# Packed tables of tiles and two register sets in the expert loops of a two-layer language-model tower

## The reference

```python
logits = xf @ Wr + br
probs = jax.nn.softmax(logits, axis=-1)
vals, idx = jax.lax.top_k(probs, K)
cw = (jax.nn.one_hot(idx, E, dtype=x.dtype) * vals[..., None]).sum(axis=1)
...
h = jax.nn.relu(xf @ W1e + b1e)
y = h @ W2e + b2e
acc + cwe[:, None] * y
```

## Time and profile before

| | us |
|---|---|
| median of 3 timed runs | 1137.43 |
| their range | 1136.9 to 1138.49 |
| span of the profiled execution | 1221.9 |
| first loop (L638 from 257.7 us on) | about 134 |
| second loop (793 to 1141.6 us) | 348.6 |

### The profile page before, as it was taken

One profiled execution on the slowest core, in us unless ns is written; L12 is line 12 of the kernel. 1 busy time (PEld: TensorE's weight loads), 2 busy tenths in 40 slices (PEclk: granted clock), 3 DMA queues, 4 the chain that ended last, 5 costly groups with the idle time before them and its releaser, 6 DMA issues.

```text
span 1221.9 us, 18019 instructions
## 1 busy us (share of the span) xinstructions
PE 802.4 (66%) x5133; PEld 637.8 (52%) x5133; DVE 778.2 (64%) x2305; ACT 437.9 (36%) x1233; POOL 510.6 (42%) x528
## 2 busy tenths in 40 slices
PE   0218963879998248778587511287887897888343
PEld 0105552679998124434255401177776787777332
DVE  7885467656665248888766699855555555666642
ACT  2543241524444134443103304533343444444200
POOL 7841001255540634662101002466664435555574
PEclk9759965579999556666665555599999998999755
DMA  2290089012221287566400404133332223333222
GB/s 69 76 403 37 1 249 309 1 50 70 71 66 38 60 143 140 118 143 131 77 1 1 132 0 127 33 85 85 89 83 81 83 77 87 88 96 94 59 72 75
DMA packets 116599, 112.95 MB, mean 92 GB/s; under 512 B 16403, under 2 KB 102994, under 8 KB 116258
## 3 DMA queue, kind: packets, MB, share of 16 engines
q1 hardware_dynamic: 103228, 84.68, 25.3%
q0 software_dynamic: 13280, 27.13, 8.2%
HBM read 76.15 MB, written 35.57 MB: 91 GB/s over the span
## 4 chain that ended last, share of the span: by engine, by line
PE 55%; DVE 22%; issue 9%; POOL 5%; ACT 4%; DMA 3%; another core or an unknown queue 1%; SPq 0%; DVEq 0%; POOLq 0%; ACTq 0%
PE ps L638 18%; PE ps L645 15%; DVE wide L1348 6%; PE ps L1969 4%; POOL wide L810 3%; PE ps L633 3%; DVE wide L1229 3%; PE ps L2231 3%; PE ps L2139 2%; PE ps L2180 2%; ACT wide L1757 2%; DVE bnst L955 2%; POOL wide L874 1%; PE ps L2076 1%; PE ps L2224 1%
## 5 line engine op out<-in xcount | busy, mean ns | idle before, releaser
L645 PE MATMUL ps<-big,wide 128*128 x1568 | 238.1, 282 | 33.9 <-ACT wide L605 20.6
L638 PE MATMUL ps<-wide 128*128 (+1 forms) x1580 | 247.1, 287 | 18.9 <-DVE wide L554 12.2
L867 POOL DMA_INDIRECT wide<-xrows,holder x189 | 182.8, 967 | 158.1 <-PE ps L633 116.1
L559 DVE TENSOR_SCALAR wide<-ps,wide 128x128 f32<-128x128 f32 x395 | 131.7, 348 | 156.9 <-PE ps L638 138.4
L638 PEld LDWEIGHTS ps<-wide 128*128 128x128 f32 x1580 | 206.2, 195 | 40.8 <-issue 32.9
L645 PEld LDWEIGHTS ps<-big,wide 128*128 128x128 f32 x1568 | 203.7, 194 | 44.5 <-issue 43.9
L605 ACT ACTIVATE wide<-ps,wide 128x128 f32<-128x128 f32 x395 | 137.8, 367 | 202.4 <-PE ps L638 184.9
L1348 DVE TENSOR_REDUCE wide<-ps 125x3 f32<-125x1500 f32 (+1 forms) x96 | 143.7, 1540 | 46.7 <-PE ps L1969 45.3
L874 POOL DMA_INDIRECT wide<-results,place x128 | 127.6, 997 | 100.1 <-DVE h L1328 44.0
L1969 PE MATMUL ps<-big 97*125 97x500 bf16 x256 | 104.8, 545 | 40.3 <-DVE wide L1348 32.5
L623 ACT COPY wide<-ps 128x128 f32<-128x128 f32 x322 | 85.2, 264 | 92.1 <-PE ps L645 78.1
(11 more groups left out here) (388 smaller groups left out, 1102.7 us busy)
## 6 DMA issues: line engine op xcount, KB each, us to landing
results<-wide SPq DMA_DIRECT2D x161, 128.0 KB, 1.8
big<-kappa SPq DMA_DIRECT2D x8, 1750.0 KB, 21.0
big<-parts SPq DMA_DIRECT2D x96, 125.0 KB
big<-in_L_ffn_W_dram SPq DMA_DIRECT2D x10, 1024.0 KB, 9.4
big<-in_L_ffn_W_dram SPq DMA_DIRECT2D x64, 128.0 KB, 2.6
parts<-wide SPq DMA_DIRECT2D x24, 250.0 KB
xrows<-wide SPq DMA_DIRECT2D x2, 1792.0 KB
wide<-results,place POOLq DMA_INDIRECT x192
```

The lines of the kernel that those rows point to most:

```text
L559: last = v.tensor_scalar(ring.hid[u % 2][:, 128 * k:128 * k + 128], ps[:, 4 + u % 2, 128 * k:128 * k + 128], w[:, hid + k:hid + k + 1], 0. ...
L638: last = t.matmul(ps[:, (2 if k < c.HC // 2 else 4) + u % 2, 128 * k:128 * k + 128], ring.w1[u % U][:, 128 * k:128 * k + 128], turned, sta ...
L645: last = t.matmul(ps[:, 6 + u % 2, 0:D], ring.hid[u % 2][:, 128 * k:128 * k + 128], w[:, D * k:D * k + D], start=k == 0, stop=k == c.HC - 1)
L867: gp.indirect_dma_start(ring.rows[j % RING], None, xrows[:, :], bass.IndirectOffsetOnAxis(ap=holder[:, j:j + 1], axis=0)).then_inc(S(f"row ...
```

## The change

The tables become bytes. PE's has two bytes per tile, the expert's number and the place of the block in the ring, unscaled; VectorE's has one byte per tile, the expert's number alone. Both are written by copies that convert to bytes; the separate scaling and the second column of VectorE's table are gone. The four tables now have places of their own in one tensor.

The loops read the bytes as 32-bit words: four words hold a round of eight tiles for PE, two for VectorE. There are two register sets; in the middle of each round (after the fourth tile on PE, in the third on VectorE) one load brings the next round's words into the set that is not in use. `value` cuts a byte out of its word, by a shift and an AND, and multiplies it by the scale.

```diff
-        table = sb("table", [1, 2 * TAB], I32)
+        table = sb("table", [1, 4 * TAB], U8)
...
         class Words:
...
+            def __init__(self, engine, p, table, tiles):
+                self.engine, self.table, self.tiles = engine, table.bitcast(I32), tiles
+                self.count = table.shape[-1] * RING // (4 * tiles)
+                self.sets = [[engine.alloc_register(f"{p}word{k}_{n}") for n in range(self.count)] for k in range(2)]
+
+            def load(self, turn):
+                at_ = turn * self.count
+                self.engine.reg_load(self.sets[turn % 2], self.table[0:1, at_:at_ + self.count])
+
+            def value(self, tile, byte, scale, top):
+                per = 4 * self.count // RING
+                word, bit = divmod(8 * (tile % RING * per + byte), 32)
+                reg = self.engine.snap(self.sets[tile // RING % 2][word])
+                field = (reg >> bit if bit else reg) & 255
+                return nc.s_assert_within(field * scale, 0, top * scale, skip_runtime_bounds_check_because="the tables hold clipped numbers")
...
-                    stage(words.value(u, 0), u + 3)
-                    if u % 2 and first_tile + u + RING < c.tiles:
-                        words.load(first_tile + RING, u - 1)
+                    if u == DVE_WORDS_AT and first_tile + RING < c.tiles:
+                        words.load(first_tile // RING + 1)
+                    if first_tile + u + 3 < c.tiles:
+                        stage(words.value(first_tile + u + 3, 0, c.wcols, c.E - 1), u + 3)
+                    else:
+                        stage(0, u + 3)
...
-                    first(u + 1, words.value(u, 1))
+                    first(u + 1, words.value(first_tile + u + 1, 1, 128, KEEP[c.n] - 1))
...
-                    second(words.value(u, 0), u)
-                    if u % 2 and first_tile + u + RING < c.tiles:
-                        words.load(first_tile + RING, u - 1)
+                    second(words.value(first_tile + u, 0, c.HC * D, c.E - 1), u)
+                    if u == PE_WORDS_AT and first_tile + RING < c.tiles:
+                        words.load(first_tile // RING + 1)
...
-                me.did(TS(tiles_[:, :, 0], one, float(c.HC * D), None, ALU.mult))
-                me.did(TS(stages_[:, 0:tab - 1, 0], one[:, 1:tab], float(c.wcols), None, ALU.mult))
-                me.then(TS(wrap, numbers, float(keep), -128.0 * keep, ALU.is_ge, ALU.mult))
-                me.did(v.scalar_tensor_tensor(stages_[:, :, 1], numbers, 128.0, wrap, ALU.mult, ALU.add))
+                me.did(v.tensor_copy(tiles_[:, :, 0], one))
+                me.did(v.tensor_copy(stage_tables[f], one))
                 me.settle()
-                me.then(TS(wrap, block, float(keep), -128.0 * keep, ALU.is_ge, ALU.mult))
-                me.then(v.scalar_tensor_tensor(tiles_[:, 0:tab - 1, 1], block[:, 1:tab], 128.0, wrap[:, 1:tab], ALU.mult, ALU.add))
+                me.then(TS(wrap, block, keep, -keep, ALU.is_ge, ALU.mult))
+                me.then(TT(out=tiles_[:, :, 1], in0=block, in1=wrap, op=ALU.add))
```

More of the change, by code:

```diff
@@ L21 @@
 U32 = mybir.dt.uint32
+U8 = mybir.dt.uint8
 ALU = mybir.AluOpType
@@ L94 @@
 KEEP = {0: 32, 1: 67}
+PE_WORDS_AT = 3
+DVE_WORDS_AT = 2
 def ap(t, offset, dims):
@@ L261, in tower_kernel @@
         b1r = sb("b1r", [128, 2, 128])
-        table = sb("table", [1, 2 * TAB], I32)
+        table = sb("table", [1, 4 * TAB], U8)
         w0 = 2 * FFN[0].tab
-        assert 2 * w0 <= 2 * TAB <= 512
-        tile_tables = [table[0:1, 0:w0], cst[0:1, 128:128 + 2 * TAB].bitcast(I32)]
-        stage_tables = [table[0:1, w0:2 * w0], table[0:1, 0:2 * TAB]]
+        assert w0 % 16 == 0 and w0 + FFN[0].tab <= TAB
+        tile_tables = [table[0:1, 0:w0], table[0:1, TAB:3 * TAB]]
+        stage_tables = [table[0:1, w0:w0 + FFN[0].tab], table[0:1, 3 * TAB:4 * TAB]]
         place = [sb("place", [128, 4, NT], I32)] * 2
@@ L457, in weight_loads @@
             return c.E // (8 if c.n else 4) + (W2_EARLY if c.n else 8)
[L459 to L467, removed]
@@ L469, in tower_kernel @@
-        class Words:
[L471 to L482, removed]
+        class Words:
+            def __init__(self, engine, p, table, tiles):
[11 more added lines that the diff above has]
+                return nc.s_assert_within(field * scale, 0, top * scale, skip_runtime_bounds_check_because="the tables hold clipped numbers")
@@ L484, in free @@
             def free(self):
-                for r in self.regs:
+                for r in self.sets[0] + self.sets[1]:
                     self.engine.free_register(r)
@@ L565, in expert_vector @@
             dve.wait_ge(S(f"w{c.n}_ld"), 16 * weight_loads(c))
-            w1, _ = pairs_of(mybir.EngineType.DVE, stage_tables[c.n], 0, 2, (c.E - 1) * c.wcols, (KEEP[c.n] - 1) * 128)
-            words = Words(dve, p, stage_tables[c.n], 2, (c.E - 1) * c.wcols, (KEEP[c.n] - 1) * 128)
+            words = Words(dve, p, stage_tables[c.n], c.tab)
+            words.load(0)
             dve.wait_ge(S("bank_filled"), nfill[at[f"holder{c.n}", len(c.parts) - 1]])
@@ L571, in expert_vector @@
             v.tensor_copy(ring.blocks[:, 0:128], ps[:, 0, 0:128]).then_inc(S(p + "blocks_in"), 1)
-            stage(w1[0], 1)
+            stage(words.value(1, 0, c.wcols, c.E - 1), 1)
             dve.wait_ge(S(p + "turned"), 2)
             v.tensor_copy(ring.blocks[:, 128:256], ps[:, 1, 0:128]).then_inc(S(p + "blocks_in"), 1)
-            stage(w1[1], 2)
+            stage(words.value(2, 0, c.wcols, c.E - 1), 2)
             dve.wait_ge(S(p + "hid_filled"), 3)
@@ L647, in second @@
                 last.then_inc(S(p + "res_filled"), 1)
-            words = Words(pe, p, tile_tables[c.n], 0, (c.E - 1) * c.HC * D, (KEEP[c.n] - 1) * 128)
+            words = Words(pe, p, tile_tables[c.n], c.tab)
+            words.load(0)
             pe.sem_inc(S(p + "hid_filled"), 2)
@@ L1152, in route @@
                 dve.wait_ge(S("emptied_dve"), nth[at[f"expert{f}", 0]])
-                keep = KEEP[f]
+                keep = float(KEEP[f])
                 numbers = tileno[0:1, 0:tab]
-                tiles_, stages_ = (t_.rearrange("o (t w) -> o t w", w=2) for t_ in (tile_tables[f], stage_tables[f]))
+                tiles_ = tile_tables[f].rearrange("o (t w) -> o t w", w=2)
+                me.did(TT(out=block, in0=numbers, in1=one, op=ALU.subtract))
                 if f:
-                    me.did(TT(out=block, in0=numbers, in1=one, op=ALU.subtract))
                     me.then(TS(second, one, float(c.E), None, ALU.is_ge))
```

2 lines of the change are left out of this document (removed).

## The result

The changed kernel takes 1154.37 us (median of 4, 1152.27 to 1156.91) against 1137.16 for the kernel before (median of 4, 1131.89 to 1138.49): a ratio of 1.0157, 95% interval 1.0129 to 1.0185. So it is slower by about 17 us, in the range and on the side that was forecast, and by more than the point forecast of +3.9 us.

What follows compares the result with a forecast made beforehand. No engine was full throughout; PE's products bound the first loop, and its sequencer lengthened undisturbed second-loop tiles. Terms +6.2 + 1.1 - 2.4 - 1.0 = +3.9 us on 1137.4 gave 1141 us, range 1125 to 1163.

Steps and rivals of the forecast that it cites:

- The price c: Both loops, PE's sequencer: one added register instruction costs 0.09 us, four 0.36 us per tile; range 0.085 to 0.105.
- sign of five to six register instructions per tile: PE's sequencer: five to six register instructions per tile in place of three would show the forecast right.
- What a tile took before: Second loop, kernel before: undisturbed tiles average 1.03 us in tiles 79 to 140 and 1.00 in 141 to 251.
- Tiles 79 to 140: Second loop, 62 tiles, 47 turning a block: PE's sequencer needs 1.13 us against 1.03 before, +6.2 us.
- Tiles 141 to 251: Second loop, 111 tiles without a turn: PE's sequencer needs 1.01 us against 1.00 before, +1.1 us.
- Tiles 0 to 78: Second loop: PE's sequencer would need 1.16 us, hidden under POOL's 1.25 us a block; 0.
- the third rival: Second loop is POOL's in the timed execution, hiding the sequencer's work: 1136 us, chance 0.20.
- The starts and the tables: Ahead of both loops, fewer loads before PE's first turn, -2.4 us; table building, two DVE instructions fewer, -1.0 us.
- VectorE in the loops: Both loops: its two added instructions and its 0.34 us load in one tile of eight have slack; 0.
- Cheap instructions: Rival, PE's sequencer: register instructions near the lower bound of 0.05 us each; 1124 us, chance 0.28.
- Dear ones: Rival, PE's sequencer: register instructions at the upper bound, c = 0.12 us each; 1164 us, chance 0.16.
- The first loop: First loop, 70 tiles: PE's products fill 1.89 us a tile and cover the sequencer's 1.4 us; cost 0.

Runs made afterwards that it cites:

- PE alone: Kernel before with only TensorE's table packed as in the change, VectorE keeping its table of 32-bit offsets: 1156.35 us, ratio 1.0174 to the kernel before.
- the second AND: Changed kernel with another AND (of 127, altering no value) behind each value on PE: 1197.76 us, ratio 1.0524 to the kernel before.
- second profile of the kernel before: Kernel before, without an edit, profiled once more: 1127.84 us in that execution, span 1126.1 us, second loop 279.5 us.

## Why the prediction held in its range and missed in size

The mechanism was right: four register instructions per tile on PE's sequencer, in a loop where that sequencer has little slack, cost more than three saved loads give back. PE alone shows the whole loss, and the second AND shows that the price is paid in full. The range, from a gain of 12 us to a loss of 26, was wide, and the side owes something to luck: two errors of the sum nearly cancel, and most of the loss is two things that it had at nothing, the hold-ups of a full sequencer and the first part of the second loop. By the prediction's steps:

**The price c.** I took 0.09 us as the price of one. The AND costs that (0.086 in time, 0.092 in the trace), but the shift costs 0.12, and the four come to 0.41 us a tile where I had 0.36: 0.05 too little, 8.7 us over 173 tiles. At 0.10 each the price still lies in the range that I gave for c. (My sign of five to six register instructions per tile was miscounted: three and four more are seven.) The reason that I gave for going below the rows, that timed executions are quicker than traced ones, fell with the stalls: the changed kernel's profile and its time agree.

**What a tile took before.** I read 1.03 and 1.00 us as undisturbed. The second profile of the kernel before shows the steady pattern, here L638 in the tail:

```profile
1004.84 0.71 PE L638 MATMUL ps<-wide 128*128 x4
1005.83 0.61 PE L638 MATMUL ps<-wide 128*128 x4
1006.95 0.71 PE L638 MATMUL ps<-wide 128*128 x4
1007.94 0.61 PE L638 MATMUL ps<-wide 128*128 x4
```

It is 0.99 and 1.12 in turn, mean 1.05, and 68.6 / 62 = 1.11 in the middle part. My tiles of the earlier trace rows stood just behind stalls. This mistake made the loss look larger than it was, by 62 x 0.08 + 111 x 0.05 = 10.5 us, and outweighs the first. With both set right my sum would be about +2 us, which nobody could have told from no change.

**Tiles 79 to 140.** +6.2 forecast, +6.9 measured. The agreement is luck: the tile after takes 75.5 / 62 = 1.22 us, not 1.13, and the tile before 1.11, not 1.03.

**Tiles 141 to 251.** +1.1 forecast, +9.6 measured; this is the term that was mis-sized. The sequencer's 1.01 us was 0.60 + 0.41 + 0.05 = 1.06, and 126.5 us over 111 tiles is 1.14: a sequencer without time to spare is also held up for some 0.08 us a tile, for which my sum had nothing. In tiles 79 to 140 it is about 0.06, in both parts together some 12 us. The tile with a load takes 1.52 (1042.79 to 1044.31), because a full sequencer hides none of it.

**Tiles 0 to 78.** 0 forecast, under POOL's 1.25 us a block; +5.5 measured. The cover is real but lower than I put it: eight blocks are fetched ahead, so 71 gathers of 1.25 us, 88.8 us, have to fit into the part, 1.17 us for each of some 76 tiles after the start. The kernel before's tiles are mostly 1.13 us there (starts of L674), so it runs into the gathers, but late and only twice; the chain of its second profile, 838 to 858 us, shows both:

```profile
835.60 4.37 DMA wide<-xrows,holder
...
849.42 4.05 DMA wide<-xrows,holder
```

Each of these tiles takes about 1.1 us more than its neighbours, so the gathers set the pace for some 2 us only. The changed kernel's tiles are 1.15 to 1.3 and 1.6 with a load, and its sequencer never waits for a gather in this part. POOL's own waits in the second loop, before (second profile) and after, show who is ahead of whom; columns as in the earlier trace rows:

```profile
POOL wide L867 <- PE ps L633: 14.6, 32, 2.0
```

```profile
POOL wide L867 <- PE ps L632: 34.3, 61, 2.1
```

POOL waits more than twice as long for PE's turns after the change. So the third rival, a loop that is POOL's, has something for it in the first part of the kernel before only, and not after.

**The starts and the tables.** -2.4 and -1.0 forecast. PE's first turn of the first loop in the second profile of the kernel before, and after:

```profile
253.96 0.66 PE L633 MATMUL ps<-cst,wide 128*128 128x128 f32 x2 [2.65 <-issue]
```

```profile
255.57 0.66 PE L632 MATMUL ps<-cst,wide 128*128 128x128 f32 x2 [1.58 <-DVE big L1302]
```

The idle time ahead of it is 1.07 us shorter. In the second loop the stretch from the holder's copy to the first products went from 2.76 us (769.64 to 772.40) to 1.62 (776.60 to 778.22), by 1.14. The two table instructions are gone and the byte writes cost what word writes did (0.28 us for a copy of 256 values). These terms were right: 22.0 - 1.1 - 1.1 - 1.0 = 18.8, which the measured 17.2 agrees with, as its interval is 14.7 to 21.0.

**VectorE in the loops.** 0 forecast. In the changed kernel it is hidden, since PE alone costs as much as the whole. By itself it is +4.5 us against the same edit with a load that the copy doesn't wait for. I counted the load as 0.34 us, for four words; two words take 0.53 to 0.81.

**The rivals.** Cheap instructions (1124) are excluded by the 0.086 of the second AND. Dear ones (c = 0.12, 1164) had the shift's price for all four and came out 10 us too high: with 1.11 and 1.05 us for the tiles before, 62 x (1.25 - 1.11) + 111 x (1.13 - 1.05) is 17.6 where that sum had 28.0. The page "Runtime: NRT & Kernel Launch" of the Trainium skill, section "Instruction fetch mechanics", speaks of an issue floor of about 20 cycles per instruction, from which the estimate of 17 ns followed. As a price that is far too little here: the register instructions lie at 0.09 to 0.12 us. The first loop behaved as forecast: its tiles are still 1.9 us, with PE full, and from the first L637 to the last (256.5 to 390.6) it takes 134.1 us against 133.6.

## What to carry to other kernels

Where an engine's program is unrolled into short tiles, count the sequencer's instructions like products: set the sequencer's time per tile beside the engine's, and ask whether a load that is saved is paid for by arithmetic that is added. Here, from four words on, a word more in a load costs about 0.07 us ((1.18 - 0.33) / 12), and a byte cut out of a word costs two instructions, 0.18 to 0.21 us, so offsets that are ready to use are better than packed ones on the engine that is the limit; packing paid here on VectorE alone, which had time to spare, and there by 3 us, outside the loops. And one profile is one execution: if its span and the timed runs differ by 7%, take a second one before reading a tile from it.

## What the runs showed of the hardware that was not expected

- A load of table words into registers takes 0.54 us for two words, 0.33 for four, 0.59 to 0.82 for eight and 0.68 to 1.29 for sixteen on PE. On VectorE two take 0.52 to 0.81 and four 0.34. Why two take longer than four stays open. The Trainium skill, page "Runtime: NRT & Kernel Launch", section "Instruction fetch mechanics", gives about 200 ns per register for TENSOR_LOAD, which that page describes as loading registers from HBM; the loads here, from SBUF, don't agree, with 0.08 us a register at four.
- A register instruction that runs for 0.032 us (the AND) holds PE's sequencer for 0.092, a move of 0.029 for 0.09 and a shift of 0.06 for 0.12.
- One profiled execution had stalls of 1 to 2 us in every third or fourth tile, 69 us in the loop, and another of the same kernel had hardly any. What caused them was not tried.
